# Softmax sums of an attention block: inverted in a reshaped copy that goes through DRAM, and read back as factors

## What is computed

```
x = x + layernorm(attention(layernorm(x)))     # 16 heads of 16, causal, rotary q and k
x = x + layernorm(ffn(layernorm(x)))           # rank 64 up and down, 1024 wide, gelu
```

```
attn = softmax(scores masked above the diagonal)
out  = attn @ v
out @ proj_w.T + proj_b
```

## Time and profile before

| | |
|---|---|
| median of 3 runs | 1461.18 us |
| the profiled execution | 1475.42 us, span 1473.7 us |
| PE busy | 1321.4 us, 90% |
| DVE busy | 1129.2 us, 77% |
| ACT busy | 890.9 us, 60% |
| POOL busy | 626.1 us, 42% |
| mean granted clock of TensorE | 0.891 of full speed |
| DMA | 140.87 MB, 96 GB/s |

### The profile page before, as it was taken

One profiled execution on the slowest core, in us unless ns is written; L12 is line 12 of the kernel. 1 busy time (PEld: TensorE's weight loads), 2 busy tenths in 40 slices (PEclk: granted clock), 3 DMA queues, 4 the chain that ended last, 5 costly groups with the idle time before them and its releaser, 6 DMA issues.

```text
span 1473.7 us, 29171 instructions
## 1 busy us (share of the span) xinstructions
PE 1321.4 (90%) x11888; PEld 584.0 (40%) x11888; DVE 1129.2 (77%) x1652; ACT 890.9 (60%) x1228; POOL 626.1 (42%) x564
## 2 busy tenths in 40 slices
PE   6689889989899989998999899889999989899995
PEld 2234334434434334343444344434343434345442
DVE  5688776779588878796678868887788687856856
ACT  4337565556466656665666666655566566777784
POOL 3363213842177216731483248422861131324444
PEclk9779678978799889998997999879998897999997
DMA  6735333455326643653466335743554345022322
GB/s 204 162 90 123 59 59 52 124 112 112 56 77 134 116 62 60 152 115 54 56 154 135 62 52 127 162 67 52 110 129 86 59 84 133 24 80 84 103 72 71
DMA packets 93066, 140.87 MB, mean 96 GB/s; under 512 B 19078, under 2 KB 55044, under 8 KB 92932
## 3 DMA queue, kind: packets, MB, share of 16 engines
q1 hardware_dynamic: 92932, 139.01, 44.7%
HBM read 70.79 MB, written 50.33 MB: 82 GB/s over the span
## 4 chain that ended last, share of the span: by engine, by line
PE 48%; DVE 17%; SPq 10%; DMA 10%; issue 6%; ACT 5%; POOL 3%; ACTq 0%; DVEq 0%; POOLq 0%
PE PV L1064 12%; PE RING L1046 8%; DMA SUM<-OT 8%; PE RING L1019 6%; SPq L886 5%; PE MI L983 5%; DVE SUM L1213 4%; DVE M L1192 4%; PE RING L1115 3%; PE MI L1074 3%; PE RING L1108 3%; DVE MB L1192 3%; ACT PB L1399 2%; DMA X<-x 2%; SPq L908 2%
## 5 line engine op out<-in xcount | busy, mean ns | idle before, releaser
L1399 ACT ACTIVATE PB<-RING 128x1024 f32<-128x1024 f32 (+2 forms) x640 | 586.6, 938 | 311.3 <-PE RING L1046 305.2
L1192 DVE TENSOR_REDUCE M<-RING 128x2 f32<-128x1024 f32 (+3 forms) x448 | 500.6, 1143 | 127.8 <-PE RING L1019 88.1
L1046 PE MATMUL RING<-QK 50*128 50x512 f32 (+3 forms) x1536 | 315.2, 443 | 45.0 <-DVE M L1192 17.6
L1019 PE MATMUL RING<-QK 48*128 48x512 f32 (+3 forms) x1536 | 305.4, 426 | 24.6 <-ACT PB L1399 10.9
L1472 POOL TENSOR_SCALAR_AFFINE_SELECT PB<-PB 128x512 f32<-128x512 f32 x256 | 164.7, 646 | 293.9 <-ACT PB L1399 293.7
L1064 PE MATMUL PV<-PB,VL 128*32 128x512 f32 (+3 forms) x2048 | 267.4, 610 | 15.7 <-ACT OT L1405 13.9
L1192 DVE TENSOR_REDUCE MB<-RING 128x2 f32<-128x768 f32 (+2 forms) x192 | 198.2, 1040 | 83.9 <-PE RING L1026 83.2
L1046 PEld LDWEIGHTS RING<-QK 50*128 50x128 f32 x1536 | 145.9, 201 | 265.5 <-DVE M L1192 97.9
L1019 PEld LDWEIGHTS RING<-QK 48*128 48x128 f32 x1536 | 159.2, 211 | 166.1 <-ACT PB L1399 93.4
L1477 POOL TENSOR_TENSOR ATT<-ATT,SUM 128x512 f32<-128x512 f32 x32 | 40.8, 1274 | 258.4 <-DVE SUM L1213 258.4
L1213 DVE RECIPROCAL SUM<-SUM 128x512 f32<-128x512 f32 x32 | 107.1, 3347 | 13.9 <-DMA SUM<-OT 13.7
(11 more groups left out here) (117 smaller groups left out, 1356.9 us busy)
## 6 DMA issues: line engine op xcount, KB each, us to landing
QK<-split_parts SPq DMA_DIRECT2D x372, 128.0 KB, 6.0
split_parts<-PARTS SPq DMA_DIRECT2D x60, 256.0 KB, 3.0
split_parts<-EO SPq DMA_DIRECT2D x60, 256.0 KB, 3.4
ATT<-OT SPq DMA_DIRECT2D x128, 64.0 KB, 2.6
block_mid<-Y SPq DMA_DIRECT2D x16, 512.0 KB, 9.5
F_X<-block_mid SPq DMA_DIRECT2D x16, 512.0 KB, 5.7
out<-F_Y SPq DMA_DIRECT2D x32, 256.0 KB, 2.2
X<-x SPq DMA_DIRECT2D x7, 1024.0 KB, 9.7
```

The source lines that it names most:

```text
L1019: ins = e.matmul(m[:, h, i, :], QK[g % 3][r, 0, k, 128 * t:128 * t + 128], QK[g % 3][r, 1, k, k0:k0 + n], start=(i == 0), stop=not open_en ...
L1046: ins = e.matmul(m[:, h, i, :], QK[g % 3][r, 1, k, 128 * j:128 * j + 128], QK[g % 3][r, 0, k, 512 * c + off:512 * c + 512], start=True, st ...
L1192: e.tensor_reduce(acc, ring(("max", g, s, u), pairs, n), AX.X, ALU.max).then_inc(v_max, 1)
L1399: e.activation(buf[:, :, pairs[0]:pairs[-1] + 1, :], ring(("score", g, s, u), pairs, n), ACT.Exp).then_inc(a_exp, 1)
```

## The change

Of the 16 equal rows of sums per head only one is kept. `att_load` writes it, for the four heads of the group, to a tensor in DRAM (`head_sums`, two DMAs of two rows of 2 KB), in place of the three DMAs to `SUM[c]`. After the fourth group of a batch there are three new steps on the SP queue and a smaller inversion, once per batch and half (16 times in all):

- `att_sums` reads the 16 heads by 512 sums of a half back as 128 partitions of 2 by 32 (one DMA, 32 KB, pieces of 128 bytes);
- `att_inverse` inverts 128x64 on DVE, once in place of twice 128x512;
- `att_out` writes the inverses to DRAM (`inverse_sums`, one DMA, 32 KB, pieces of 128 bytes);
- `att_spread` reads them back to the tile `INV` (128 by 2 by 512), each head's row to 16 partitions (two DMAs of 256 KB). `INV` is one tile for both halves.

`att_scale` keeps its size and its number, but both parts of a half are now scaled one behind the other at the end of the batch, with `INV`. `att_load` waits for the inversion of the batch before in place of the scaling of two groups before. Planned costs and due times are given for the new steps; the planner then makes a new order for all engines.

```diff
@@ due_times
-                if g % 2:
-                    at += [(z + 2.5, ("att_inverse", g // 4, c, g % 4 // 2)), (z + 3, ("att_scale", g // 4, c, g % 4 // 2))]
+                if g % 4 == 3:
+                    at += [(z + 1 + i / 2, (n, g // 4, c)) for i, n in enumerate(("att_sums", "att_inverse", "att_out", "att_spread"))]
+                    at += [(z + 3, ("att_scale", g // 4, c, k)) for k in range(2)]
@@ needs
-        return [("ot_copy", g, c), ("att_scale", (g // 2 - 1) // 2, c, (g // 2 - 1) % 2), ("proj", g // 4 - 1, c, 2)]
-    if what == "att_inverse":
-        b, c, k = at
-        return [("att_load", 4 * b + 2 * k + 1, c)]
+        return [("ot_copy", g, c), ("att_inverse", g // 4 - 1, c), ("proj", g // 4 - 1, c, 2)]
+    if what in ("att_sums", "att_inverse", "att_out", "att_spread"):
+        b, c = at
+        last = (b, 0) if c else (b - 1, 1)
+        return {"att_sums": [("att_load", 4 * b + i, c) for i in range(4)] + [("att_spread", b - 1, c)],
+                "att_inverse": [("att_sums", b, c), ("att_out", b - 1, c)],
+                "att_out": [("att_inverse", b, c), ("att_scale", b - 1, c, 1)],
+                "att_spread": [("att_out", b, c), ("att_scale", *last, 1)]}[what]
@@ COST and MOVES (ns; bytes, bytes per ns, ns)
-        "rope": 2400, "round": 750, "rest": 2360, "att_scale": 1300, "att_inverse": 650, "f_norm": 1000, "f_res": 1250,
-        "load_x": 600, "send": 3300, "load_group": 5600, "shift": 2500, "store": 500, "att_load": 3000, "f_load": 5000, "f_fill": 3000,
+        "rope": 2400, "round": 750, "rest": 2360, "att_scale": 1300, "att_inverse": 550, "f_norm": 1000, "f_res": 1250,
+        "load_x": 600, "send": 3300, "load_group": 5600, "shift": 2500, "store": 500, "att_load": 2400, "att_sums": 600, "att_out": 600, "att_spread": 1200, "f_load": 5000, "f_fill": 3000,
...
-         "shift": (1 << 15, 150, 1500), "att_load": (5 << 16, 200, 1500), "store": (1 << 19, 230, 4200),
+         "shift": (1 << 15, 150, 1500), "att_load": (1 << 17, 200, 1500), "att_sums": (1 << 15, 150, 1500),
+         "att_out": (1 << 15, 150, 1500), "att_spread": (1 << 19, 200, 2500), "store": (1 << 19, 230, 4200),
@@ sync, att_load
-                    if g >= 2:
-                        w.wait_ge(g_att, NTH["att_scale", (g // 2 - 1) // 2, c, (g // 2 - 1) % 2])
                     if g >= 4:
+                        w.wait_ge(v_inv, NTH["att_inverse", g // 4 - 1, c])
                         w.wait_ge(p_mi["proj"], NTH["proj", g // 4 - 1, c, 2])
...
-                    for r, p0, n in ((0, 0, 16), (16, 48, 32), (48, 112, 16)):
-                        e.dma_start(SUM[c][r0 + r:r0 + r + n, :], OT[p0:p0 + n, :]).then_inc(s_att[c], 16)
+                    for h, p0 in ((0, 0), (1, 48)):
+                        h0 = 4 * (g % 4) + h
+                        e.dma_start(sums[c, h0:h0 + 3:2, :], OT[p0:p0 + 65:64, :]).then_inc(s_att[c], 16)
+                elif what == "att_sums":
+                    b, c = at
+                    w.wait_ge(s_att[c], 64 * (4 * b + 4))
+                    e.dma_start(SUM[c][:, :, :], sums[c].rearrange("(k h) (j q) -> (h j) k q", k=2, q=32)).then_inc(s_sum[c], 16)
+                elif what == "att_out":
+                    b, c = at
+                    w.wait_ge(v_inv, NTH["att_inverse", b, c])
+                    if b:
+                        w.wait_ge(g_att, NTH["att_scale", b - 1, c, 1])
+                    e.dma_start(inverse[c].rearrange("(k h) (j q) -> (h j) k q", k=2, q=32), SUM[c][:, :, :]).then_inc(s_inv[c], 16)
+                elif what == "att_spread":
+                    b, c = at
+                    w.wait_ge(s_inv[c], 16 * (b + 1))
+                    if b or c:
+                        w.wait_ge(g_att, NTH["att_spread", b, c] * 2 - 2)
+                    for k in range(2):
+                        src = inverse[c, 8 * k:8 * k + 8, :].unsqueeze(1).broadcast_to([8, 16, 512])
+                        e.dma_start(INV[:, k, :], src).then_inc(s_spread, 16)
@@ vector
-                    w.wait_ge(s_att[c], 80 * (4 * b + 2 * k + 2))
-                    e.reciprocal(SUM[c][:, :], SUM[c][:, :]).then_inc(v_inv, 1)
+                    w.wait_ge(s_sum[c], 16 * (b + 1))
+                    e.reciprocal(SUM[c][:, :, :], SUM[c][:, :, :]).then_inc(v_inv, 1)
@@ scalar, ot_copy
-                    w.wait_ge(s_att[1 - c], 80 * (g + c))
+                    w.wait_ge(s_att[1 - c], 64 * (g + c))
@@ gpsimd, att_scale
-                    w.wait_ge(v_inv, NTH["att_inverse", b, c, k])
-                    e.tensor_tensor(ATT[c][:, k, :], ATT[c][:, k, :], SUM[c][:, :], ALU.mult).then_inc(g_att, 1)
+                    w.wait_ge(s_spread, 32 * NTH["att_spread", b, c])
+                    e.tensor_tensor(ATT[c][:, k, :], ATT[c][:, k, :], INV[:, k, :], ALU.mult).then_inc(g_att, 1)
```

More of the change, by code:

```diff
@@ L287, in needs @@
         g, c = at
-        return [("ot_copy", g, c), ("att_scale", (g // 2 - 1) // 2, c, (g // 2 - 1) % 2), ("proj", g // 4 - 1, c, 2)]
-    if what == "att_inverse":
-        b, c, k = at
-        return [("att_load", 4 * b + 2 * k + 1, c)]
+        return [("ot_copy", g, c), ("att_inverse", g // 4 - 1, c), ("proj", g // 4 - 1, c, 2)]
[6 more added lines that the diff above has]
+                "att_spread": [("att_out", b, c), ("att_scale", *last, 1)]}[what]
     if what == "att_scale":
-        return [("att_inverse", *at)]
+        return [("att_spread", *at[:2])]
     if what == "proj":
@@ L380 @@
         ("POOL", "ones ln_pow select att_scale y_pow residual f_pow f_ypow"),
-        ("SP", "load_x send load_group shift att_load store f_load f_fill f_rest f_next f_store")):
+        ("SP", "load_x send load_group shift att_load att_sums att_out att_spread store f_load f_fill f_rest f_next f_store")):
     TAKER.update(dict.fromkeys(names.split(), engine))
@@ L581, in block_kernel @@
     split = nc.dram_tensor("split_parts", (2, 2, 2, 16, 16, NT), fp32, kind="Internal").ap()
+    sums, inverse = (nc.dram_tensor(n, (2, 16, 512), fp32, kind="Internal").ap() for n in ("head_sums", "inverse_sums"))
     mid = nc.dram_tensor("block_mid", (NB * NT, D), fp32, kind="Internal").ap()
@@ L648, in block_kernel @@
             ATT = [sb(f"ATT{c}", [128, 2, 512]) for c in range(2)]
-            SUM = [sb(f"SUM{c}", [128, 512]) for c in range(2)]
+            INV = sb("INV", [128, 2, 512])
+            SUM = [sb(f"SUM{c}", [128, 2, 32]) for c in range(2)]
             YS = [sb(f"Y{i}", [128, 4, D]) for i in range(2)]
@@ L711, in block_kernel @@
         s_mid = [sem(f"s_mid{i}") for i in range(2)]
-        s_att = [sem(f"s_att{c}") for c in range(2)]
+        s_att, s_sum, s_inv = ([sem(f"s_{n}{c}") for c in range(2)] for n in ("att", "sums", "inverse"))
+        s_spread = sem("s_spread")
         v_half, v_one, v_pv0, v_bvw, v_mask = (sem(f"v_{n}") for n in ("half", "row", "pv_zero", "bias_wide", "mask"))
```

## The result

| | before | after |
|---|---|---|
| median | 1463.03 us (4 runs, 1460.17 to 1468.82) | 1413.88 us (4 runs, 1411.27 to 1435.04) |
| ratio, 95% interval | | 0.9653 (0.961 to 0.9696) |
| span of the profiled execution | 1473.7 us | 1410.8 us |
| PE busy | 1321.4 us | 1252.2 us |
| DVE busy | 1129.2 us | 1048.3 us |

The kernel is 3.5% faster, 49 us by the medians and 51 by the ratio; forecast were 28 us, 1433 us.

The account below looks back on a forecast made before the run. PE was taken to bound attention, busy 1098.0 of 1200 us. Gains of 39 us less costs of 3.5, 1.5 and 6 gave 28, scaled to 27.7: 1433 us from 1461.18; own range 1415 to 1450, whole range 1400 to 1470.

Parts of the forecast that it names:

- rival 3: All the chain of waits holds of the inversions returns, 51 us, plus 10 of clock: 1401 us; chance 0.15.
- Rival 2: The inversions were hidden anyway, DVE's gain becomes waiting for PE: 1461 us, within 4; chance 0.11.
- the 8 places where the rows showed a stall: Half 0's second inversions in front of `chain_a`: four places return 15.6 us, the other four 4 us.
- the other 22: Remaining inversions, with no loss beside them in the rows: floor nothing, ceiling 23 us, 11 taken.
- 8 + 7 = 15: First inversions: 8 us at half 0's stalls at 146 and 310 us, 7 from the other 22.
- the new chain's waits: Waits caused by the DRAM trip at each half's end: costs of 3.5, 1.5 and 6 us.
- At `proj`: PE waits for half 0's scalings, a us late in half of the batches: 6 us with the clock.
- The loads: Each group's load is 0.6 us shorter, at most 38 us less latency, nearly all hidden: counted as nothing.
- The clock: Fewer stretches at 1.2 GHz in attention: mean clock 0.90 to 0.92, PE's idle time from 102 to about 85 us.
- Rival 1: Factors come late and PE waits in front of `proj`, 8 stalls of 5 to 6 us: 1497 us; chance 0.19.
- The half-engine rule: `att_spread` has 8 heads outermost, so half the DMA engines carry it; scalings about 2 us later, sum 1449 us.
- 8 us either way: Allowance, without a sign, for the planner's new lists on all engines after costs and due times changed.

Follow-up runs that it names:

- e1: Kernel before with its own order and DMAs, each inversion cut from 512 to 64 columns: 1409.7 us, ratio 0.9665.
- e4: Changed kernel with 448 more columns inverted on DVE, unread, in one piece behind each of the 16 small inversions: 1454.2 us, ratio 0.9936.
- e5: Kernel before with only the 16 second inversions cut to 64 columns: 1425.9 us, ratio 0.9789 to the kernel before.
- e6: Kernel before with only the 16 first inversions, in mid-batch, cut to 64 columns: 1438.1 us, ratio 0.9884.
- e9: Changed kernel without the DMAs of the way through DRAM, factors set to ones: 1430.1 us, ratio 0.9702 to the kernel before.
- e3: Kernel before without the third of the three DMAs that load SUM in each att_load: 1449.1 us, ratio 0.9935.
- e10: Changed kernel with each att_spread issued again after SP waits for the first to land, factors some 5 us later: 1522.0 us, ratio 1.0405.
- e7: Kernel before with inversions cut to 64 columns, in the order planned with an inversion cost of 3350 ns, not 650: 1515.6 us, ratio 1.0389.
- e12: Changed kernel with two OT tiles and the addition of eps moved from DVE to POOL: 1396.7 us, ratio 0.9563 to the kernel before.

## Where the prediction was right and where it was not

**Direction, range and bound: right, the size too small.** PE is the bound and the time came back through PE. 1413.9 us lies in the whole range, 1400 to 1470, and 1 us below the forecast's own, 1415 to 1450. It is 19 us from the forecast and 13 from rival 3, 1401. Rival 2 (hidden anyway) is out by e1.

**Rival 3 was nearer in its first item than the forecast.** It gave back all that the chain of waits holds of the inversions, 59 - 8 = 51 us; e1 measured 49 and the change 51. Its second item, 10 us more of clock, did not come. That the chain's share was the better measure here than the sum by places is one case, and no run shows why.

**The mechanism: right.** e1 shows that taking away DVE's time in the inversions alone gives as much as the change, and with it the wait for the negated maxima falls from 15.5 to 0.7 us. e4 shows that a block of 2.9 us, put back behind the inversions, takes most of the gain away. The second inversions, among them the 8 places where the rows showed a stall and "a stretch at 1.2 GHz that costs as much again", hold the larger part (e5). How the loss splits between stall and clock is another matter, below.

**The gains by place: a term that was too small, by 10 us.** For the second inversions 15.6 + 4 us and their share of "the other 22", 8 of 22 x 11 = 4: 24 us; e5 measured 31, from 24 to 37. For the first 8 + 7 = 15; e6 measured 17. Together 39 forecast, 49 measured in e1 (40 to 58). The middle values put most of what was missing to the second inversions, 7 us, and 2 to the first, each within its interval. Which item was off, the 8 places in front of `chain_a` or "the other 22", of which 8 are second ones, no run separates: the ceiling of the other 22, 50 in all, would fit, and so would a larger loss at the visible places. My guess is that part of a stall's price comes later than the ten us that I looked at.

**The costs: a term that was too large.** 3.5 + 1.5 + 6 = 11 us were taken off for the new chain's waits. Measured: without the trip (e9) the kernel isn't faster, and at most 6 us fit into the intervals. Singly: DVE's wait for the sums was put at 15 to 35 us and is 2.7; at the place shown the inversion starts 3.7 us behind the issue of `att_sums`, with no wait. At `proj` I had 6 us; POOL's scalings end 1.2 us ahead of it at the place shown, and no wait of PE for them is in the list. For SP's waits I had 1.5 us, and PE's wait for `QK<-NSROW` is 1.2, though SP stood for 123 us in all in front of the three new steps. That the change has e1's ratio to 0.001 does not prove that nothing was lost: it has 9 us less of inversions on DVE than e1 (8.7 and 17.5) and shorter loads. The chain itself was sized right, 13.6 us against 14.3.

**The loads: counted as nothing,** while e3 gives 9 us for one DMA fewer. Whether the change has that too can't be said: e1's 49 and this 9 would be 58, and 51 were measured.

**The clock: 0.90 to 0.92 forecast, 0.95 measured; PE's idle time to 85 us forecast, 107 measured.** Here the picture was wrong, not only its size: the gain came as busy time. In e1, the same gain came as 30 us of idle time and 36 of busy time, against the same trace of before. How a list of work divides its losses between idle time and clock I can't predict from these traces.

**Rival 1: it did not happen, and its price is open.** I had the factors' lateness decide from a spread of 7 us in place of 4.5; no run stands near that point. At 5 us late the rival said 1497 us, and e10 took 1522. But e10 also makes SP wait: the waits for `QK<-NSROW` are 27.9 us, those at `proj`, which are the rival's own, are 2 of 11.0 us in all, where it had 8 of 5 to 6. So the rival's way of losing time took less in e10 than it said, and SP's queue, which it left out, took more.

**The half-engine rule.** The sentence on the Trainium skill's "DMA: Bandwidth & Descriptors", section "Why a DMA increments its semaphore by 16 and not by 1", had 8 of 16 engines for the spread. Two stretches in its middle, and one in a load of queries and keys behind it (the last column but one is the share of the 16 engines):

```profile
356.50:357.50 1.00, 1.00 (x9) 0.16 (x8) 1.00 (x2) 0.90 (x2) 0.00 (x0) 1.00 0.50 193
357.50:358.50 1.00, 1.00 (x18) 0.65 (x14) 0.56 (x2) 0.13 (x1) 0.00 (x0) 1.00 0.52 193
...
364.00:365.00 1.00, 1.00 (x24) 0.61 (x20) 1.00 (x1) 0.41 (x1) 0.52 (x1) 1.00 0.99 143
```

The share is 0.50 and 0.52: by that rule, the trace agrees. It cost nothing at this place, because the whole spread, with half of the engines, had landed by 359.85, when the scaling starts, 5.2 us behind its first issue at 354.64; I had put 1.2 + 4.5.

**The order: "8 us either way" was no bound.** e7 shows that one cost number can move the time by 106 us. For the change's own order no run stands alone: order, loads and chain together make 2 us against e1, give or take 11.

## What to carry to other kernels

Where one engine is busy 90% of the time and its clock falls behind stalls, look in the lists of the engines that feed it for long single instructions ahead of something it waits for, and not only for the largest sum: 16 blocks of 2.9 us cost 41 us here, and more work than that in pieces of 0.84 us, most of them elsewhere, cost 14. Whether length or place did it was not told apart. A round trip through DRAM of 14 us cost nothing that could be measured in an order that had been planned with it; a wait of 4 us in the DMA queue for its own transfer, 16 times, with the factors 5 us later, cost 110 us. And when a hand-made order comes from a cost table, measure after each number that you correct.

## What was not expected of the hardware

- DVE's 128x4 and 128x32 instructions took 0.1 to 0.2 us or, some of them, 1.1 to 2.3 us, at the place shown until the end of a 128x1024 operation that POOL had begun just ahead. DVE's busy time fell by 81 us and not by the 98 that the inversions gave back; 17 of it are in two of these groups, `VE` from 3.2 to 12.6 and `YNM` from 5.0 to 13.0 us.
- Taking away a stall of PE need not pay: with the five gaps of 2.3 us gone (e12), time and clock did not improve.
